# One relu of every fourth pair in two float32r parts, with the subtraction on GpSimd

## The reference, cut to what matters

```python
h = relu(layernorm(x))                                   # 3125 x 256
node_i, node_j = h[i_idx], h[j_idx]                      # i_idx = src, j_idx = dst, 50000 each
msg_input = concatenate([node_i, node_j, edge_features], axis=-1)
hid = relu(msg_input @ mW1 + mb1)                        # 50000 x 512
messages = hid @ mW2 + mb2
aggregated = segment_sum(messages, i_idx)                # 3125 x 256
# then the update network, its residual, and a three-layer graph convolution
```

## Time and profile before

| what | value |
|---|---|
| three runs | 2032.16, 2037.77, 2036.21 us; median 2036.21 |
| profiled execution | 2026.99 us, its span 2025.3 us |
| TensorE busy over the span | 1810.6 us (89%) |
| VectorE | 1544.2 us (76%) |
| GpSimd | 1256.3 us (62%) |
| ScalarE | 797.6 us (39%) |
| granted TensorE clock, mean | 0.925 of full speed |

### The profile page before, as it was taken

How to read it: one execution, slowest core, us unless ns; L and a number is a source line. 1 busy time by engine, 2 the same in 40 slices (tenths; PEclk the granted TensorE clock), 3 DMA queues, 4 the chain that set the end, 5 groups by cost and what they waited for, 6 DMA issues and landing times. The chain is left out here.

```text
span 2025.3 us, 34940 instructions
## 1 busy us (share of the span) xinstructions
PE 1810.6 (89%) x9004; PEld 1239.8 (61%) x9005; DVE 1544.2 (76%) x4663; ACT 797.6 (39%) x1975; POOL 1256.3 (62%) x1468
## 2 busy tenths in 40 slices
PE   3577877777499999999999998999989999999999
PEld 3344444444255555555555556777758788888887
DVE  8877776777489999999999988999987445445333
ACT  0122222222155566665655555666664222103000
POOL 4777777777788888888888859999977100000000
PEclk7677777888699999999999999999999999999999
DMA  5111111111276666666666696222226233333333
GB/s 166 39 59 50 53 58 52 57 59 58 61 200 198 196 196 194 196 196 196 196 195 195 197 182 172 74 72 73 88 85 199 94 113 121 109 125 110 109 109 111
DMA packets 181291, 254.03 MB, mean 125 GB/s; under 512 B 28876, under 2 KB 144265, under 8 KB 181098
## 3 DMA queue, kind: packets, MB, share of 16 engines
q0 software_dynamic: 48048, 126.51, 22.7%
q1 hardware_dynamic: 104408, 102.03, 16.2%
q10 hardware_dynamic: 28642, 23.25, 3.6%
HBM read 202.22 MB, written 49.37 MB: 124 GB/s over the span
## 5 line engine op out<-in xcount | busy, mean ns | idle before, releaser
L1037 POOL DMA_INDIRECT brow<-B_rows,rows x440 | 470.0, 1068 | 115.2 <-issue 61.5
L393 POOL DMA_INDIRECT src_list<-ring,ring_row x392 | 385.4, 983 | 133.8 <-issue 116.8
L2018 PE MATMUL pO<-F,y 128*128 128x512 f32 x1728 | 427.7, 401 | 0.8 <-DVE y L1822 0.8
L2018 PEld LDWEIGHTS pO<-F,y 128*128 128x128 f32 x1728 | 325.1, 189 | 73.7 <-ACT zT L1911 1.5
L1360 POOL TENSOR_SCALAR src_oh<-iota,src_s 128x128 bf16<-128x128 bf16 x426 | 279.2, 672 | 32.4 <-PE pC L1512 15.8
L1087 PE MATMUL pNode<-hid_whole,oh 128*128 128x512 f32 x440 | 227.4, 598 | 4.2 <-DVE sums L1223 3.7
L1153 ACT ACTIVATE turned<-pC 128x256 fp32r<-128x256 bf16 x220 | 84.4, 384 | 280.4 <-PE pC L1066 280.4
L1376 DVE TENSOR_SCALAR dst_oh<-iota_cw,dst_s 128x458 bf16<-128x458 f16 x568 | 182.5, 370 | 1.6 <-PE pC L1512 1.4
L1512 PE MATMUL pC<-dst_oh,src_oh 128*128 128x458 bf16 x568 | 159.9, 361 | 18.4 <-SPq L1467 11.3
L1089 PE MATMUL pNode<-hid_upper,oh 128*128 128x512 f32 x220 | 174.9, 795 | 0.0
L852 PE MATMUL pP<-U,upto 128*128 128x182 bf16 x385 | 48.9, 277 | 136.4 <-DVE posf L612 136.4
(11 more groups left out here) (308 smaller groups left out, 3423.6 us busy)
## 6 DMA issues: line engine op xcount, KB each, us to landing
raw<-C_rows SPq DMA_DIRECT2D x54, 768.0 KB, 4.3
C_rows<-c_rows ACTq DMA_DIRECT2D x175, 114.5 KB, 1.7
raw_first<-C_rows SPq DMA_DIRECT2D x18, 768.0 KB, 4.2
rows<-src_list SPq DMA_DIRECT2D x110, 100.0 KB, 2.8
brow<-B_rows,rows POOLq DMA_INDIRECT x440, 3.8
U_parts<-part_u SPq DMA_DIRECT2D x25, 256.0 KB, 2.0
B_rows<-bst SPq DMA_DIRECT2D x25, 256.0 KB, 2.1
src_list<-ring,ring_row POOLq DMA_INDIRECT x392, 2.2
```

What stands on the lines that cost most here:

```text
L393: nc.gpsimd.indirect_dma_start(dr.src_list[:, :, :].rearrange("p t w -> (p t) w"), bass.IndirectOffsetOnAxis(ap=ring_row[:, k % RING, t:t ...
L1037: nc.gpsimd.indirect_dma_start(brow[:, t % BR, :], None, dr.B, bass.IndirectOffsetOnAxis(ap=rows_i[:, m % LCS, j, 1:2], axis=0)).then_inc( ...
L2018: last = mm(pO[m % 2][half][:, :], y[:, win, part, half * P:(half + 1) * P], F[:, n % FS, :], start=(win == 0 and part == 0), stop=False)
```

## The change

In every fourth pair (p % 4 == 3, 55 of 220) the first tile is handled as the second is. ScalarE writes, besides `whole`, a float32r relu `upper_a`. GpSimd subtracts it from `whole`, as float32r, into `lower_a`. TensorE then issues two float32r matmuls, with `upper_a` first and `lower_a` last of the pair's four, in place of the float32 one. GpSimd makes the subtraction of pair p ahead of the first gather of pair p + 5, behind that gather's own wait for `pre`. The last two, of pairs 215 and 219, come behind its loop. `whole` has two places instead of three. The integers 0 to 457, which had a tile of their own, now lie in the second place of `pre`, and VectorE waits before it writes there until it has read them.

```diff
-        WHOLE, SPLIT = 3, 2
+        WHOLE, SPLIT = 2, 2
+        BOTH = 4
...
+        upper_a = g.sb("hid_upper_a", [P, HID], F32R)
+        lower_a = g.sb("hid_lower_a", [P, HID], F32R)
...
-        iota_i = g.sb("iota_cw_i", [P, CW], I32)
+        iota_i = pre[:, 1, 0:CW].bitcast(I32)
...
@@ GpSimd
+            def lower_part_a(p):
+                pool.wait_ge(whole_ready, p + 1)
+                pool.wait_ge(upper_ready, p + 1)
+                if p >= BOTH:
+                    pool.wait_ge(node_done, p - BOTH + 1)
+                nc.gpsimd.tensor_tensor(lower_a[:, :], whole[:, p % WHOLE, :], upper_a[:, :].bitcast(F32), ALU.subtract
+                                        ).then_inc(lower_a_ready, 1)
...
                 if t >= BR:
                     pool.wait_ge(pre_ready, (t - BR) // 2 + 1)
+                p = t // 2 - BR // 2 - 1
+                if t % 2 == 0 and p >= 0 and p % BOTH == BOTH - 1:
+                    lower_part_a(p)
                 nc.gpsimd.indirect_dma_start(
...
+            for p in range(NT // 2 - BR // 2 - 1, PAIRS):
+                if p % BOTH == BOTH - 1:
+                    lower_part_a(p)
             pool.wait_ge(ub_added, NW)
@@ TensorE, node(p)
-                pe.wait_ge(whole_ready, p + 1)
-                mm(pN[p % 2][:, :], oh[:, q % OHQ, j, :].bitcast(F32), whole[:, p % WHOLE, :], start=True, stop=False)
+                both = p % BOTH == BOTH - 1
+                if both:
+                    pe.wait_ge(upper_ready, p + 1)
+                    mm(pN[p % 2][:, :], oh[:, q % OHQ, j, :], upper_a[:, :], start=True, stop=False)
+                else:
+                    pe.wait_ge(whole_ready, p + 1)
+                    mm(pN[p % 2][:, :], oh[:, q % OHQ, j, :].bitcast(F32), whole[:, p % WHOLE, :],
+                       start=True, stop=False)
...
-                mm(pN[p % 2][:, :], oh[:, q % OHQ, j + 1, :], lower[:, p % SPLIT, :], start=False, stop=True
-                   ).then_inc(node_done, 1)
+                last = mm(pN[p % 2][:, :], oh[:, q % OHQ, j + 1, :], lower[:, p % SPLIT, :], start=False,
+                          stop=not both)
+                if both:
+                    pe.wait_ge(lower_a_ready, p // BOTH + 1)
+                    last = mm(pN[p % 2][:, :], oh[:, q % OHQ, j, :], lower_a[:, :], start=False, stop=True)
+                last.then_inc(node_done, 1)
@@ ScalarE, behind the relu into whole
+                    if p % BOTH == BOTH - 1:
+                        nc.scalar.activation(upper_a[:, :], pre[:, p % 2, 0:HID], ACT.Relu)
@@ VectorE, add_target(p)
+                if p == 1:
+                    dve.wait_ge(consts, KT + 2)
```

More of the change, by code:

```diff
@@ L992, in edge_mlp @@
         lower_ready = g.sem("lower_ready")
+        lower_a_ready = g.sem("lower_a_ready")
         node_done = g.sem("node_done")
```

## The result

The changed kernel takes 2092.86 us (2089.69 to 2094.54, 3 runs) against 2036.21, a ratio of 1.0287 [1.0258, 1.0317]. The profiled execution took 2089.69 us with a span of 2088.0, so 62.7 more than the one of before. The forecast was 2098, and 2089 in the terms of the profiled execution.

What follows compares the result with a forecast made beforehand. TensorE was taken as the bound at 11.81 us a round; GpSimd's subtraction would make it 12.97. 53 x 1.16 = 61 and 1 at the end on 2027 give 2089, plus 9.2 for the median: 2098 us, range 2060 to 2140 (8 in 10).

Steps and rivals of the forecast that it cites:

- The bound before: Edge stage, 600 to 1180 us: TensorE bounds the kernel, busy 579.69 of 580.00 us, with a round of 11.81 us.
- GpSimd's free sixth: GpSimd in the edge stage: its idle time is fixed pieces of 0.30 and 0.16 us, counted as part of each gather.
- The subtraction: 1.30: GpSimd's added 128x512 subtraction from two SBUF inputs: 1.30 us, estimated from the 128x256 `resid` add's median of 0.740.
- The round: 12.5 and 13.4, mean 12.97: GpSimd's round of four pairs after the change: 12.44 us, or 13.4 with a `resid` add; mean 12.97 including 0.05 for waits.
- the layout: Hand-made schedule of one round from a subtraction's end, placing gathers, copies, `pre`, `hid_lower` and one-hots; every second round has `resid`.
- TensorE's wait of 1.3 us: Before the last matmul of each fourth pair, TensorE stands about 1.3 us per round for GpSimd's subtraction; VectorE waits with it.
- rival 3: Subtraction and `hid_lower` hold each other: subtraction 1.9 us or more, round about 13.9, 112 us added, 2148 us; chance 0.09.
- TensorE's share 88%: Expected sign between 600 and 1180 us: TensorE's busy share falls to about 88% at a clock of 1.00.
- rival 4: TensorE, standing a tenth of its time, is granted 1.2 GHz in places; one round in ten adds about 50 us; chance 0.03.
- Rival 1: It ends faster: with a 0.70 us subtraction GpSimd's round is 11.2, under TensorE's 11.41, giving 2015 us; chance 0.06.
- The other edits: `whole` with two places, 55 more relus, the iota in `pre` and VectorE's wait: hidden or put at nothing, except at the end.
- The end: 1.2 us late: After the last subtraction, ending at 1210.2, two copies of about 1.5 us make the turns of the lists 1.2 us late.

## Why the prediction was right, point by point

- **The bound before.** Right: TensorE. In the repeat of the kernel before its matmuls idle 0.03 us a round (578.52 of 580 us busy). But the trace on which the prediction rests was at the quick end of that kernel. Between the two repeats the round grows by 12.89 - 11.99 = 0.90 us, not by 1.17, and the spans by 45.8. The 9.2 us that the forecast adds for that quick trace are, for the changed kernel, 3.2 (2092.86 against 2089.69); the forecast's 5 us too many come from there.
- **GpSimd's free sixth is not free.** Right for this execution, and the repeat shows how much was there: 0.66 us a round. The prediction had a round between 10.22 and 11.86 "at the upper end only because it has time to"; that is what the repeat confirms.
- **The subtraction: 1.30.** It took 1.28.
- **The round: 12.5 and 13.4, mean 12.97.** It was 12.33 and 13.30, mean 12.98. The mean is closer than the layout deserves, and that is luck: each kind of round is 0.1 to 0.2 us shorter than laid out, but the long kind came in 35 of 52 rounds and not in every second. The order differs: the copy was not held (0.20, not to 11.14), and the time went into the gathers behind the subtraction. Rounds of 13.3 also came where no `resid` was added.
- **TensorE's wait of 1.3 us, before the fourth matmul.** The amount is about right (1.12 us a round), the place is not. Two thirds stand one pair later, at `sums`. The step that failed is the free run of VectorE in the layout: it had the one-hot at 10.4 to 11.1, clear of the subtraction. This is rival 3's mechanism, with the one-hot in the place of `hid_lower`. Its price of 112 us did not come, since the hold lengthened VectorE and TensorE, which had over 1 us a round to spare, and not GpSimd: 1.28 in all 50. The prediction's last sentence names as a sign of being wrong that "TensorE waits for anything else"; this sign came, for 0.77 of the 1.12 us. Another expected sign did not: VectorE's waits for the edge matmuls from 600 to 1180 us did not grow but fell, from 38.3 to 28.7 us, which fits the held one-hots.
- **TensorE's share 88%.** It was 91%: 529.96 of 580, or 11.86 us a round where the prediction had 11.41. The waits that its matmuls show are not all: the weight loads ahead of them stood 63.4 us for `sums` in the window, the matmuls 34.6, and the first matmul behind a wait is recorded longer (1.12 instead of 1.02, 0.49 instead of 0.40).
- **The clock.** 1.00 throughout; rival 4 did not come. At the other end, 0.40 us less per float32 matmul is right too: the four half matmuls of a later pair end at 805.25, 805.48, 805.71 and 805.95, 0.23 apart.
- **Rival 1's point of decision was wrong.** It gave 2015 us for a subtraction below 0.89 us. With none at all the time is 4 us less at best, not 22. I had taken TensorE's 11.41 as the next floor and had not laid out VectorE, which needs 3.1 to 3.5 us from a one-hot to the end of `sums`, against the 2.55 us of TensorE's shortened pair. This cost the prediction nothing, since the case had 0.06, but by the timelines of the runs without a subtraction on GpSimd it is why none of them was faster.
- **The other edits: nothing.** Right but for the end: the run without subtractions has the two places of `whole`, the iota in `pre` and the extra relus, and takes the time of before.
- **The end: 1.2 us late.** It was 2.1. The subtraction began 0.14 us behind its input's end at 1270.31 and took 1.72 instead of 1.30; the two copies took less than was put, 1.24 instead of 1.5. The rest lies on the other side: the pair's extra relu makes the input itself later. TensorE was free 0.97 us behind it (1271.28), where the prediction had 1210.44 - 1208.87 = 1.57.

No version that was run beats the kernel before by more than its interval.

## What to carry to other kernels

An engine with idle time between its instructions may still be out of room. Count the pieces: if each is the fixed gap between two instructions and none is a wait, an instruction added there costs about its full length (here 1.17 us a round for 1.28), whatever it saves elsewhere. Before paying for a saving on the engine that sets the pace, find the next floor by laying out the engine one step behind it, here VectorE through two PSUM banks. The saving fell in one pair of four, and the timelines show it lost again at the next pair's wait for one of two banks.

## What was not expected of the hardware

- Issue order did not protect VectorE. The one-hot, recorded 0.41 us ahead of the subtraction, ended 0.56 us behind it, at 2.25 instead of 0.69 us, while GpSimd ran at its normal 1.28. In other runs the hold went the other way: the subtraction of half the width took 713 to 1259 ns for the same 256 columns, and the full one 1.67 us behind a `hid_lower` recorded 0.16 us ahead. What decides it was not tried.
- A gather that begins inside a VectorE instruction with two SBUF inputs ends a fixed time behind it. In the trace of before the 182 gathers that begin well inside a `hid_lower` all end 0.82 to 0.85 us after it, and so last from 1.04 to 1.40 us. With one input from PSUM they take 0.95. The Trainium skill ("SBUF — State Buffer", section "Who interferes with whom") infers that the making of descriptors goes free beside a `tensor_tensor` with two SBUF inputs. The runs disagree, for gathers that begin inside: behind the one-hot, which is such a one, 84 gathers of the run with `hid_lower` from PSUM end 0.82 to 0.90 us after it. One already under way is not lengthened. The gather also takes its row numbers from `rows` in SBUF; whether that read or the making of descriptors is held was not separated.
- On two of three chips the same kernel took 7 to 8% longer, 146 to 165 us. Most of that lies ahead of the edge stage, which starts 119 to 129 us later in the traces of the variants. Inside it there are signals of TensorE up to 4 us late, mostly in the variants with the subtraction on GpSimd. The cause of both is open. The ratios measured there can't be carried over: the subtraction with no reader cost 1.0131 on one of them and 1.0231 on the chip like the first.
